# Decoder kernel, second grouped attention: value product from three 128-row matmuls on a block-diagonal P

## What is computed

```
# N_Q = 32 query heads, N_KV = 8 key and value heads, head size 128, SLIDE = 64 = N tokens
q = (x @ wq.T).reshape(B, N, 32, 128).transpose(0, 2, 1, 3)
k = (x @ wk.T).reshape(B, N, 8, 128).transpose(0, 2, 1, 3)
v = (x @ wv.T).reshape(B, N, 8, 128).transpose(0, 2, 1, 3)
s = einsum('bhgnd,bhmd->bhgnm', q grouped by 4, k) / sqrt(128); masked to j <= i
p = softmax(s, axis=-1)
o = einsum('bhgnm,bhmd->bhgnd', p, v)
return o.reshape(B, N, 32 * 128) @ wo.T
```

## Time and profile before

| | us |
|---|---|
| median of 3 runs | 1708.49 (1708.4 to 1709.02) |
| the profiled execution, its own time | 1707.01 |
| span in its trace | 1705.2 |
| TensorE busy in the span | 1596.9 (94%) |
| VectorE busy | 983.1 (58%) |
| ScalarE busy | 659.7 (39%) |
| GpSimd busy | 202.9 (12%) |
| mean granted TensorE clock | 0.979 of full |

### The profile page before, as it was taken

One profiled execution on the slowest core, in us unless ns is written; L12 is line 12 of the kernel. 1 busy time (PEld: TensorE's weight loads), 2 busy tenths in 40 slices (PEclk: granted clock), 3 DMA queues, 4 the chain that ended last, 5 costly groups with the idle time before them and its releaser, 6 DMA issues. The chain is left out here.

```text
span 1705.2 us, 22804 instructions
## 1 busy us (share of the span) xinstructions
PE 1596.9 (94%) x8526; PEld 1277.1 (75%) x8526; DVE 983.1 (58%) x1946; ACT 659.7 (39%) x1191; POOL 202.9 (12%) x146
## 2 busy tenths in 40 slices
PE   8788689999999999999889999999999999979998
PEld 6565477788778778876777788788878877757866
DVE  5897757756676676667433542552553446246645
ACT  4666424433443443334333332332332323336541
POOL 8421130000000000000340000000000000703330
PEclk9999899999999999999999999999999999999999
DMA  5110011100110110100111110110110100202221
GB/s 211 50 44 26 15 48 38 62 26 27 50 50 1 51 62 13 38 13 26 45 51 38 38 50 9 53 52 10 49 62 12 37 13 25 79 6 83 77 80 50
DMA packets 26023, 75.44 MB, mean 44 GB/s; under 512 B 3888, under 2 KB 4624, under 8 KB 25680
## 3 DMA queue, kind: packets, MB, share of 16 engines
q1 hardware_dynamic: 25552, 73.16, 12.9%
q0 software_dynamic: 384, 1.05, 0.2%
HBM read 72.10 MB, written 2.10 MB: 44 GB/s over the span
## 5 line engine op out<-in xcount | busy, mean ns | idle before, releaser
L83 PE MATMUL bankY<-sb_Dwo,sb_DoT 128*128 128x512 f32 x768 | 193.4, 401 | 0.3 <-DVE sb_DoT L1033 0.3
L83 PE MATMUL bankY<-sb_Bwo,sb_BoT 128*128 128x512 f32 x768 | 193.3, 401 | 0.2 <-DVE sb_BoT L1033 0.2
L83 PE MATMUL bankA<-sb_xT,sb_Bwq 128*128 128x512 f32 x768 | 190.1, 397 | 0.0
L83 PE MATMUL bankA<-sb_xT,sb_Dwq 128*128 128x512 f32 x768 | 189.9, 396 | 0.0
L83 PEld LDWEIGHTS bankY<-sb_Dwo,sb_DoT 128*128 128x128 f32 x768 | 140.6, 189 | 42.4 <-issue 13.6
L83 PEld LDWEIGHTS bankY<-sb_Bwo,sb_BoT 128*128 128x128 f32 x768 | 140.8, 189 | 42.1 <-issue 13.2
L83 PEld LDWEIGHTS bankA<-sb_xT,sb_Dwq 128*128 128x128 f32 x768 | 142.2, 188 | 34.1 <-issue 2.7
L83 PEld LDWEIGHTS bankA<-sb_xT,sb_Bwq 128*128 128x128 f32 x768 | 142.3, 188 | 33.7 <-issue 2.4
L964 DVE TENSOR_TENSOR sb_BqT<-bankA,sb_Btable 128x512 f32<-128x512 f32 x64 | 44.2, 691 | 151.6 <-ACT sb_Bsw L866 151.6
L1000 DVE TENSOR_TENSOR sb_xtok<-sb_xtok,bankY 128x512 f32<-128x512 f32 x128 | 87.1, 680 | 53.7 <-PE bankY L83 53.6
L866 ACT ACTIVATE sb_Bsw<-bankA 64x512 f32<-64x512 f32 x160 | 94.8, 593 | 54.8 <-PE bankA L83 51.7
(11 more groups left out here) (277 smaller groups left out, 2987.1 us busy)
## 6 DMA issues: line engine op xcount, KB each, us to landing
sb_raw<-in_w_attn SPq DMA_DIRECT2D x80, 512.0 KB, 3.4
sb_raw<-in_q_gu SPq DMA_DIRECT2D x22, 256.0 KB, 2.7
sb_raw<-in_q_d SPq DMA_DIRECT2D x11, 256.0 KB, 2.7
sb_rawx<-in_xT SPq DMA_DIRECT2D x4, 512.0 KB, 6.5
sb_raw<-in_wqk SPq DMA_DIRECT2D x8, 256.0 KB, 2.6
sb_xtok<-in_x_tok SPq DMA_DIRECT2D x1, 2048.0 KB, 11.9
sb_raw<-in_ctxT SPq DMA_DIRECT2D x4, 512.0 KB, 3.8
sb_raw<-in_ctx_tok SPq DMA_DIRECT2D x4, 512.0 KB, 3.8
```

The lines of the kernel that those rows point to most:

```text
L83: last = nc.tensor.matmul(out, lhs, rhs, start=start and i == 0, stop=stop and i == len(pairs) - 1)
```

## The change

For D alone (full = not rope) the value product is made as the other products are: V and the transposed P are split in high and low parts of type fp32r, and one product() of three matmuls with 128 rows and 512 columns replaces the two float32 matmuls of 64 rows and 256 columns. For that, pt holds P of both batches block-diagonally: batch 0 in rows 0 to 63 and columns 0 to 255, batch 1 in rows 64 to 127 and columns 256 to 511, the rest zero. GpSimd writes the zeros once (8 memsets of 64 rows and 256 columns, behind kt's), and TensorE's slots, ScalarE's and VectorE's start wait for them (p_zero). ScalarE copies P in two instructions of 64 rows; VectorE makes the low parts in two more (probabilities_low) ahead of the slot's softmax steps. The low part of V is made on VectorE too (values_low): four times at the start, then in the VALUES_AT slots behind the weight blocks and ahead of the late slots' front(u+2). v_done is now given by values_low. In every slot but 0 and 8 the output product now stands ahead of the value product. The result lies in one bank of bankO, in turns, instead of half of both.

```diff
@@ -643,6 +643,7 @@
...
+    p_zero = sem("G_pzero"); p_low = sem("G_plow"); v_high = sem("G_vhigh")
...
@@ -662,9 +663,16 @@
-            V = sb(mem, f"{tag}V", [P, NT, 2 * HD])
+            full = not rope
+            if full:
+                V = [sb(mem, f"{tag}V{i}", [P, NT, 2 * HD], F32R) for i in range(2)]
+                pt = [[sb(mem, f"{tag}pt{i}{p}", [P, 2, GROUP * S], F32R) for p in range(2)] for i in range(2)]
+            else:
+                V = sb(mem, f"{tag}V", [P, NT, 2 * HD])
+                pt = [sb(mem, f"{tag}pt{i}", [P, GROUP * S]) for i in range(2)]
+            of_batch = lambda b: slice(S * b, S * b + S)
+            o_bank = lambda u: bankO[:, u % 2, :].rearrange("p (b h q) -> p b h q", b=2, h=GROUP) if full else bankO[:, :, 0:GROUP * S].rearrange("p b (h q) -> p b h q", h=GROUP)
...
-            pt = [sb(mem, f"{tag}pt{i}", [P, GROUP * S]) for i in range(2)]
...
@@ -719,6 +727,14 @@
+                            if full:
+                                pool.wait_ge(padded, first // NPAIR + 1)
+                                pool.wait_ge(w_low, part.weights + n + 1)
+                                for b in range(2):
+                                    for i in range(2):
+                                        for p in range(2):
+                                            nc.gpsimd.memset(f32(pt[i][p][of_batch(b), 1 - b, :]), 0.0).then_inc(p_zero, 1)
+                                    pool.wait_ge(p_zero, 4 * (b + 1))
...
@@ -805,28 +821,35 @@
+                        if full:
+                            pe.wait_ge(p_zero, 8)
...
+                            if full:
+                                pe.wait_ge(p_low, (part.it - first) * SLOTS + u + 1)
...
-                            if late(u):
+                            if late(u) or (full and u % NT):
...
-                            for b in range(2):
-                                rows = slice(S * b, S * b + S)
-                                done = nc.tensor.matmul(bankO[:, b, 0:GROUP * S], V[rows, u % NT, u // NT * HD:(u // NT + 1) * HD], pt[u % 2][rows, :], start=True, stop=True)
+                            if full:
+                                pe.wait_ge(p_low, (part.it - first) * SLOTS + u + 3)
+                                done = product(bankO[:, u % 2, :], three([v[:, u % NT, u // NT * HD:(u // NT + 1) * HD] for v in V], [p[:].rearrange("p b c -> p (b c)") for p in pt[u % 2]]))
+                            else:
+                                for b in range(2):
+                                    done = nc.tensor.matmul(bankO[:, b, 0:GROUP * S], V[of_batch(b), u % NT, u // NT * HD:(u // NT + 1) * HD], pt[u % 2][of_batch(b), :], start=True, stop=True)
...
-                            if u % NT and not late(u):
+                            if u % NT and not late(u) and not full:
...
@@ -870,7 +893,7 @@
-                        nc.scalar.activation(V[:, i:i + 2, :].rearrange("p t n -> p (t n)"), bankA[part.buffer(("V", n))][:], ACT.Copy).then_inc(v_done, 1)
+                        nc.scalar.activation((V[0] if full else V)[:, i:i + 2, :].rearrange("p t n -> p (t n)"), bankA[part.buffer(("V", n))][:], ACT.Copy).then_inc(v_high if full else v_done, 1)
...
@@ -893,6 +916,8 @@
+                        if full:
+                            act.wait_ge(p_zero, 8)
...
@@ -912,7 +937,11 @@
-                            nc.scalar.activation(pt[u % 2][:], bankT[u % 2][:, 0:GROUP * S], ACT.Copy).then_inc(pt_done, 1)
+                            if full:
+                                nc.scalar.activation(pt[u % 2][0][of_batch(0), 0, :], bankT[u % 2][of_batch(0), 0:GROUP * S], ACT.Copy)
+                                nc.scalar.activation(pt[u % 2][0][of_batch(1), 1, :], bankT[u % 2][of_batch(1), 0:GROUP * S], ACT.Copy).then_inc(pt_done, 1)
+                            else:
+                                nc.scalar.activation(pt[u % 2][:], bankT[u % 2][:, 0:GROUP * S], ACT.Copy).then_inc(pt_done, 1)
...
@@ -921,7 +950,7 @@
-                                                 bankO[:, :, 0:GROUP * S].rearrange("p b (h q) -> p b h q", h=GROUP), ACT.Copy).then_inc(o_high, 1)
+                                                 o_bank(u), ACT.Copy).then_inc(o_high, 1)
...
@@ -1002,6 +1031,19 @@
+                    def probabilities_low(part, u):
+
+                        dve.wait_ge(pt_done, part.unit(u) + 3)
+                        nc.vector.tensor_tensor(pt[u % 2][1][of_batch(0), 0, :], bankT[u % 2][of_batch(0), 0:GROUP * S], f32(pt[u % 2][0][of_batch(0), 0, :]), ALU.subtract)
+                        nc.vector.tensor_tensor(pt[u % 2][1][of_batch(1), 1, :], bankT[u % 2][of_batch(1), 0:GROUP * S], f32(pt[u % 2][0][of_batch(1), 1, :]), ALU.subtract).then_inc(p_low, 1)
+
+                    def values_low(part, n):
+
+                        i = n % 4 * 2
+                        dve.wait_ge(v_high, (part.it - first) * 4 + n + 1)
+                        nc.vector.tensor_tensor(V[1][:, i:i + 2, :].rearrange("p t n -> p (t n)"), bankA[part.buffer(("V", n))][:],
+                                                f32(V[0][:, i:i + 2, :]).rearrange("p t n -> p (t n)"), ALU.subtract).then_inc(v_done, 1)
+
...
@@ -1011,6 +1053,11 @@
+                        if full:
+                            dve.sem_inc(p_low, 2)
+                            dve.wait_ge(p_zero, 8)
+                            for n in range(4):
+                                values_low(part, n)
...
@@ -1024,18 +1071,22 @@
+                            if full:
+                                probabilities_low(part, u)
...
-                            nc.vector.tensor_tensor(oT[u % 2][1][:].rearrange("p h b q -> p b h q"), bankO[:, :, 0:GROUP * S].rearrange("p b (h q) -> p b h q", h=GROUP),
+                            nc.vector.tensor_tensor(oT[u % 2][1][:].rearrange("p h b q -> p b h q"), o_bank(u),
...
+                            if full and u in VALUES_AT and not part.final:
+                                values_low(part, VALUES_AT[u])
...
```

## The result

The changed kernel takes 1738.12 us (median, 1737.07 to 1739.17) against 1708.76 us of the kernel before in the same session: a ratio of 1.0172, 95% interval 1.0157 to 1.0186, some 29 us slower. The profiled execution took 1738.81 us with a span of 1737.0 us, against 1705.2 us before. Behind D both kernels take the same 249 us. Ahead of D, where the change does nothing, the trace of the kernel after is 2.2 us longer (D starts at 873.0 and not at 870.9 us); over all traces of this document that start lies between 866.1 and 875.5 us.

A forecast was written before the change was run, and what follows sets the result against it. TensorE was taken to bound stage D, so its added work or waits are paid in full. Stream -6.4, waits +13.8 and +12.1, start +3.1 and +1.6, tail +1.2: +25.4 on 1708.5 gives 1733.9 us, range 1724 to 1747.

The forecast's parts named there:

- rival A: The forecast itself for the whole kernel: 1733.9 us, within 1727 to 1741; chance 0.64.
- The stream: TensorE's matmuls in D: new value product 0.70 us against 0.82, 0.11 saved in each of 58 slots, -6.4 us.
- Rival C: New value product keeps the price around it, 0.89 against 0.82 us: +4 in place of -6.4, 1744 us; chance 0.08.
- The sum by columns alone: Value product by the skill's rules, 1536 columns against 1024: some 0.2 us more a slot, some 1752 us.
- Cover behind O: Usual slots: P's low part ready 1.5 us behind T, hidden by S and O; without cover about 0.4 a slot.
- Slots 0 and 8: Value product straight behind S waits for VectorE's subtractions behind a weight block: 8 x 1.73 = +13.8 us.
- Slots 10 and 14: In three turns the mask stands behind values_low and holds up Q: 6 x 2.0 = +12.1 us.
- rival B: The six 2.0 us waits also take TensorE's clock down, about 1.6 us each: 1744 or some 1750; chance 0.12.
- a sign that it is wrong: Listed signs: V waiting in other slots, the clock falling at the 2.0 us waits, or a usual slot not shorter.
- The start: D's start: first values copy waits for 8 memsets, third value projection +3.1 us, half clock behind it about +1.6.
- VectorE's work: VectorE's busy time in D grows by some 60 us with overlap, with no time of its own.
- The tail: Last turn, slots 10 to 15: rounds of 5.16 against 4.7 us, waits of 1 to 2 us for oT, +1.2 us.

The follow-up runs named there:

- the float32 run: Changed kernel with one float32 matmul of 128 rows and 512 columns, high parts only, in place of the three fp32r matmuls: 1744.41 us, one execution.
- after_again: The changed kernel measured once more, unedited, beside the others on one chip: ratio 1.0173 to the kernel before.
- the start repaired: Changed kernel with ScalarE and VectorE waiting for the zeros of P at the end of D's start, not ahead of the first values copy: ratio 1.0108.
- The order alone: Kernel before with only the output product ahead of the value product in all slots of D but 0 and 8: ratio 1.0001.
- The three repairs: Changed kernel with mask ahead of values_low, zeros waited for at the start's end, value product behind query projection in slots 0 and 8: ratio 1.0000.

## Why the prediction was right, and where it wasn't

The forecast of 1733.9 us lay 4.2 us under the time, 1738.1, inside its range; sign and mechanism are those of rival A. By its steps:

- **What bounds the kernel.** Right. Each wait added in D is paid in full: the ledger closes with waits, clock and stream alone.
- **The stream.** Right in sign, too small. I read the price ahead of the old product as 0.99 - 0.91 = 0.08, with the 0.91 from a late slot. But there the scores stand straight behind the old product, so the 0.91 already held the price behind it. In the kernel after the same 8 scores take 0.82 us in slot 4. The old product took 0.17 + 0.63 + 0.09 = 0.89 out of the stream of slot 4 and the new one takes 0.68, so the slot is 0.20 shorter and most slots 0.16 (7.49 to 7.33), not 0.11. Over 44 slots that is 7.0 where I would have had 4.8. Rival C falls: V's first weights load behind O. The sum by columns alone, 0.2 us more in a slot, falls too; the slot became 0.16 to 0.20 shorter. That changing the tiling mode costs a drain (the Trainium skill, TensorEngine Tiling (Array Packing), Key Properties) fits the float32 run, whose scores behind a product of 128 rows took 0.81 and not 0.91.
- **Cover behind O.** Right that it hides the new work, wrong about its size. P's low part is ready 2.1 us behind T (956.52 to 958.60) and not 1.5: I had left out that the subtractions wait for the end of the second copy, 0.38 us behind its start, and the second subtraction starts 0.43 behind the first, not 0.33. Without the cover a slot costs 1.1 us, as the run with V ahead of O shows, and not 0.4.
- **Slots 0 and 8.** Right: seven slots of the eight grew by 1.70 to 1.77 us, against 1.73 less 0.11 for the stream.
- **Slots 10 and 14.** Right: 1.86 to 1.94 us where the clock held, against 2.0 less 0.11.
- **The clock behind these waits.** Here the step failed that made rival B a case apart with 0.12. It was neither all nor nothing: in the eight traces that have these waits (after, after_again and six experiments) slot 10 met half clock 13 times in 24 and slot 14 2 times in 24 (both in the float32 run), at waits of 1.82 and 1.74 us; those in slots 0 and 8 (1.57 to 1.66) not once, the very first slot apart. Each fall adds about 1.6 us. That is 3.1 us in the profiled execution, and most of what the sum lacked. It belonged in the sum as a third of six falls (15 of 48), some 3 us. The prediction had named a fall at these waits as a sign that it is wrong, and two of the six showed it. That the time still lies close to the forecast is in part luck: the clock fell at few of them, and the stream's larger gain took off 2.2 us.
- **The start.** The wait (3.07 us) as predicted. The half clock behind it came too, for 6.8 us and at some 2.4 instead of 1.6: +5.5 against 3.1 + 1.6. In the first slot the value product waited 2.50 us where it had waited 0.7 before, 1.8 more, as forecast; but the clock fell a second time there, for 1.6 us. That fall was not in my sum. It stands in six of the eight traces with this wait; it is missing with the start repaired (one trace), but in the float32 run too, so what decides it stays open.
- **VectorE's work.** 72 us more busy time, where I had some 60 (128 x 0.42 and 16 x 0.69 with overlap); the two subtractions of a slot follow each other after 0.43 us and overlap hardly at all. Outside the places named it cost nothing, as said.
- **The tail.** Right: +1.4 against +1.2, with five waits for oT, of 0.3 to 1.4 us where I had said 1 to 2. The order alone makes 0.4 of it.
- **Sum.** Too low by 4.6: half clock in slot 10 3.1 and in the first slot 1.6, the start 0.8, the slots 0 and 8 together with the tail 1.2, less 2.2 for the 44 slots in which the stream saved more (rounded terms).

Not found: a version faster than the kernel before. The three repairs bring it level, and 4.4 us in slots 1 and 9 and 1.4 in the tail, with 0.6 in slots 0 and 8, stand against 6.5 in the other slots.

## What to carry to other kernels

When a product is made cheaper by splitting its operands into high and low parts, count where the new subtractions stand in VectorE's queue at the slots that are not the usual one: in the usual slot 0.85 us of new work cost nothing, while in 14 special slots and at the start it cost about five times what 44 usual ones won. The call that frees a bank goes ahead of a call that merely prepares something for later (12 us here, for the order of two calls), and a one-time preparation is waited for where it is used. To read the price of an instruction's neighbours, take the undisturbed length from a place that has no such neighbour on either side.

## What the runs showed of the hardware

- Three fp32r matmuls of 128 rows and 512 columns take 0.68 us in the stream, one float32 matmul of the same shape 0.86 us in two records, and the two float32 products of 64 rows and 256 columns in four records 0.63 us, to which 0.26 us came in their neighbours.
- Stops of 1.7 to 1.8 us between dense projections brought TensorE from full to half clock (granted clock 1.00 to 0.50) in 15 of 48 cases and cost about 1.6 us each time; stops of 1.57 to 1.66 us in the slots 0 and 8 behind the first never did. The same program met it at other places in another execution.
- Halving the rows of a copy or a subtraction saved nothing: a copy of 64x256 took 0.375 us on ScalarE (128x256 before: 0.384) and a subtraction of 64x256 0.415 us on VectorE, the mask of 128x256 0.42. Eight memsets of 64x256 on GpSimd took 2.19 us.
